# Two more score steps in the ring at the end of a pass of a Mamba, attention and experts kernel

## What is computed

```python
# L0: tokens by 64 channels -> 128 inner channels, 16 states, a scan along 1024 tokens
xh = silu(causal_conv_k2(xh, conv_w, conv_b)); dt = softplus(dt_low @ W_dt + b_dt)
h = exp(dt * A) * h + dt * B * x;  y = einsum('bdn,bn->bd', h, C) + xc * D
x = silu(group_norm((y * silu(z)) @ W_out)) + x
# L1 attention, 1024 tokens, 8 heads of 8, causal
att = softmax(mask(q @ k.T * scale)); t = t + (att @ v) @ w_proj
# L1 experts: top 2 of 8
t = t + sum over the top 2 of p_e * (ln(t) @ expert_w[e] + expert_b[e])
```

## Time and profile before

| | |
|---|---|
| median of 3 runs | 1405.29 us (1405.14 to 1409.21) |
| the profiled execution | 1405.26 us, of which its span is 1403.4 us |
| busy over the span | PE 74%, DVE 80%, ACT 49%, POOL 35% |
| granted TensorE clock, mean | 0.856 of full speed |
| largest group of DVE | L979 `row_max`, 352 instructions, 328.8 us |
| share of the chain that ended last | DVE 39%, PE 28%, of it L979 16% |

### The profile page before, as it was taken

One profiled execution on the slowest core, in us unless ns is written; L12 is line 12 of the kernel. 1 busy time (PEld: TensorE's weight loads), 2 busy tenths in 40 slices (PEclk: granted clock), 3 DMA queues, 4 the chain that ended last, 5 costly groups with the idle time before them and its releaser, 6 DMA issues.

```text
span 1403.4 us, 16864 instructions
## 1 busy us (share of the span) xinstructions
PE 1032.5 (74%) x6132; PEld 431.9 (31%) x6132; DVE 1116.6 (80%) x1398; ACT 684.2 (49%) x1178; POOL 487.1 (35%) x257
## 2 busy tenths in 40 slices
PE   3255325858886898779877998689868976986984
PEld 1001101323333333323333334233333333433442
DVE  5695359898899998999899989998999987258235
ACT  3324212438644774367446654576437702740660
POOL 3262336335442543353255334444425421000000
PEclk9557556979987999889987998899879997999895
DMA  2640583154425333534335433543154321120000
GB/s 45 165 120 31 124 169 82 40 143 123 100 64 141 97 80 90 134 91 110 72 96 125 117 82 81 123 115 81 51 135 104 81 58 41 35 50 1 2 16 8
DMA packets 40937, 120.25 MB, mean 86 GB/s; under 512 B 9222, under 2 KB 9610, under 8 KB 38475
## 3 DMA queue, kind: packets, MB, share of 16 engines
q1 hardware_dynamic: 27030, 68.83, 21.1%
q10 hardware_dynamic: 13824, 50.34, 14.4%
HBM read 95.65 MB, written 17.20 MB: 80 GB/s over the span
## 4 chain that ended last, share of the span: by engine, by line
DVE 39%; PE 28%; issue 9%; ACT 3%; POOL 2%; DMA 1%; DVEq 0%; ACTq 0%; SPq 0%
DVE row_max L979 16%; DVE state L1045 8%; PE ps L1436 6%; PE ps L1421 5%; DVE drive L1054 4%; PE ps L1304 3%; PE ps L1216 2%; PE ps L1196 2%; PE ps L1405 2%; ACT probs L866 2%; PE ps L1201 2%; DVE moe L1136 2%; PE ps L1207 1%; PE ps L1353 1%; PE ps L1424 1%
## 5 line engine op out<-in xcount | busy, mean ns | idle before, releaser
L711 POOL TENSOR_TENSOR read<-state,c_rep 128x1024 f32<-128x1024 f32 x128 | 311.3, 2434 | 365.5 <-DVE state L1045 271.9
L866 ACT ACTIVATE probs<-ps 128x512 f32<-128x512 f32 (+3 forms) x768 | 327.2, 499 | 109.2 <-PE ps L1424 79.1
L979 DVE TENSOR_REDUCE row_max<-ps 128x1 f32<-128x640 f32 (+7 forms) x352 | 328.8, 985 | 39.0 <-PE ps L1308 38.0
L1045 DVE TENSOR_TENSOR_SCAN state<-decay,drive 128x1024 f32<-128x1024 f32 x96 | 265.3, 2764 | 1.6 <-DVE drive L1054 1.2
L1421 PE MATMUL ps<-q_stack,k_stack 128*128 128x512 bf16 (+3 forms) x768 | 214.6, 345 | 65.4 <-DVE drive L1054 28.7
L1304 PE MATMUL ps<-k_stack,q_stack 128*128 128x512 bf16 (+3 forms) x704 | 200.0, 365 | 72.0 <-DVE row_max L979 70.0
L821 ACT ACTIVATE decay<-decay,a_scale 128x1024 f32<-128x1024 f32 x128 | 147.1, 1154 | 100.8 <-DMA decay<-dt_dram 100.8
L1353 PE MATMUL ps<-u_rows,pick 128*128 128x512 bf16 x256 | 113.1, 466 | 100.3 <-DVE state L1030 73.7
L1436 PE MATMUL ps<-probs,v_aug 128*32 128x512 f32 (+3 forms) x1536 | 168.2, 510 | 8.8 <-ACT probs L866 3.7
L1421 PEld LDWEIGHTS ps<-q_stack,k_stack 128*128 128x128 bf16 x768 | 75.9, 100 | 253.7 <-ACT probs L866 65.1
L1054 DVE TENSOR_TENSOR drive<-ps,b_rep 128x512 f32<-128x512 f32 x192 | 127.7, 678 | 21.0 <-PE ps L1353 19.3
(11 more groups left out here) (184 smaller groups left out, 1262.7 us busy)
## 6 DMA issues: line engine op xcount, KB each, us to landing
decay<-dt_dram ACTq DMA_DIRECT2D x96, 512.0 KB, 4.7
decay<-dt_dram SPq DMA_DIRECT2D x32, 512.0 KB, 6.1
q_stack<-q_parts_dram SPq DMA_DIRECT2D x48, 192.0 KB
k_stack<-k_parts_dram SPq DMA_DIRECT2D x48, 192.0 KB
u_rows<-read SPq DMA_DIRECT2D x96, 64.0 KB, 2.0
k_parts_dram<-read SPq DMA_DIRECT2D x40, 128.0 KB, 2.4
dt_dram<-read SPq DMA_DIRECT2D x8, 512.0 KB, 2.6
q_parts_dram<-read SPq DMA_DIRECT2D x24, 128.0 KB, 2.3
```

Source lines behind the costliest of these rows:

```text
L711: pool.tensor_tensor(read[:, k % (2 * NG), :], state[:, k % 2, :], c_rep[:, :], ALU.mult)\
L866: act.activation(probs[:, e % (2 * QUAD), 0:w], bank_of(("scores", e))[:, 0:w], ACT.Exp, scale=SCALE).then_inc(exped.sem, 1)
L979: dve.tensor_reduce(row_max[:, i, h0:h0 + nh], scores[:, :, 0:P * (i + 1)], AX.X, ALU.max, negate=True).then_inc(row_maxed.sem, 1)
L1045: dve.tensor_tensor_scan(state[:, k % 2, :], decay[:, k % DECAYS, :], drive[:, k % 3, :], 0.0, ALU.mult, ALU.add).then_inc(scanned.sem, NH)
```

## The change

`EARLY_STEPS` gets two steps more, block 2 with head 0 and block 2 with head 1, 384 columns each. The score half loses the step of block 2 with heads 0 and 1 (768 columns), so it has 43 steps where it had 44. The two new steps stand behind the last values and ahead of `heads_to_tokens(3)`. The next pass begins with two folds, the convolution, two folds and then score step 5. In `beside` nothing but the folds' steps is renumbered, so all else there stands one step earlier in the row of blocks. In the rounds half, unit 13 goes from round 9 to round 10, and f's two sets of transposes `xn_t` go from round 10 to round 8.

```diff
-        EARLY_STEPS = [(0, 0, 4), (1, 0, 2), (1, 2, 2)]
+        EARLY_STEPS = [(0, 0, 4), (1, 0, 2), (1, 2, 2), (2, 0, 1), (2, 1, 1)]
+        BEFORE_VALUES = 3
...
-                                     if quad or i > 1]
+                                     if quad or i > 2 or (i == 2 and h > 1)]
...
-        UNITS_IN = (4, 0, 2, 1, 2, 0, 2, 0, 2, 1, 2, 2, 0, 1, 2, 0, 1, 0, 1, 1, 2, 1, 2, 1, 1, 1, 0, 0)
+        UNITS_IN = (4, 0, 2, 1, 2, 0, 2, 0, 2, 0, 3, 2, 0, 1, 2, 0, 1, 0, 1, 1, 2, 1, 2, 1, 1, 1, 0, 0)
...
-        TURNS = ((0, "attn_t", 0), (1, "attn_t", 1), (2, "proj", 0), (10, "xn_t", 0), (10, "xn_t", 1),
+        TURNS = ((0, "attn_t", 0), (1, "attn_t", 1), (2, "proj", 0), (8, "xn_t", 0), (8, "xn_t", 1),
...
-                        ((1, 1), c, convolution), ((0, 2, 4, 5), p, last_folds), ((6, 8), c, gate_projection),
+                        ((1, 1), c, convolution), ((0, 0, 2, 3), p, last_folds), ((6, 8), c, gate_projection),
...
                     if p:
-                        for n in range(NEARLY):
+                        for n in range(BEFORE_VALUES):
                             early_scores(n)
                     if b:
                         add_values(NKEY - 1)
+                    if p:
+                        for n in range(BEFORE_VALUES, NEARLY):
+                            early_scores(n)
+                    if b:
                         heads_to_tokens(len(GROUPS) - 1)
```

## The result

| | before | changed |
|---|---|---|
| median of six runs | 1405.22 us (1404.09 to 1409.21) | 1397.07 us (1395.00 to 1399.73) |
| ratio, 95% interval | | 0.9937 (0.9918 to 0.9956) |
| profiled execution, span | 1405.26, 1403.4 | 1399.73, 1398.0 |
| DVE and PE busy, clock | 80%, 74%, 0.856 | 80%, 73%, 0.854 |

The direction was the forecast's, the size that of the most favourable rival, or more. The profiled execution of the changed kernel is the slowest of its six, so the two traces differ by 5.5 us only. One pair of traces must therefore not be read as the effect, and most of what follows is about telling the change from chance.

What follows compares the result with a forecast made beforehand. DVE, busy 137.0 of 150.0 us, was taken to set the pass, so only its waits could be won. Pass 3 +2.9, passes 4 to 8 -3.5, pass 9 -0.5, pass 10 -1.85: -2.95 from 1405.26, 1402.3 us, range 1398 to 1408.

Steps and rivals of the forecast that it cites:

- the most favourable rival: Whole kernel: clock in pass 3 rises as early as before, later gains come in full; -6.65, 1398.6 us; chance 0.25.
- the price in pass 3: Head of pass 3: new steps wait for scans, folds queue behind, `gate_scan` 2.2 late; 2.9 us lost (1.3 to 5.8).
- Passes 9 and 10: Score halves only: pass 9 gains 0.5 us, pass 10 gains 1.85; nothing was counted for their rounds.
- The 1.85 in pass 10's score half: Pass 10: first step of block 3 starts 1.1 earlier, value projection's wait shrinks by 0.75; 1.85 us gained (1.1 to 1.9).
- if it takes that long again it rises at 248.4: Head of pass 3: PE's clock again rises only after 5.58 us of unbroken work, making `gate_scan` 2.2 late.
- Head of passes 4 to 8: `gate_scan` starts 1.08 us earlier, but the first step of block 3 only 0.20 earlier.
- the cover by ACT's copy: Head of passes 4 to 8: new steps' 0.5 us of PE fit the 0.70 gap while ACT copies the sums.
- Score half, 0.35 a pass: Passes 4 to 8: chain from `gate_group_norm` starts 1.35 earlier, leaving 0.35 us a pass gained (0.1 to 0.60).
- Rounds half, 0.35 a pass from the wait of 0.70: Passes 4 to 8: moving unit 13 removes unit 16's 0.70 wait, unit 14 comes 0.35 later; 0.35 us a pass gained.
- All that can be won is won: Whole kernel: pass 3 costs only 1.4, passes 4 to 8 gain 0.60 and 0.50 each; -6.65, 1398.6 us; chance 0.25.
- The gains are handed back: Passes 4 to 8: later DVE waits grow by what is won, DVE's work unchanged; +0.55, 1405.8 us; chance 0.2.
- The transposes block the ring: Round 10, passes 4 to 8: units 13, 14, 15 each 0.6 late; +6.2 in all, 1411.5 us; chance 0.1.

Runs made afterwards that it cites:

- r1: The changed kernel run again, nothing altered: 1397.38 us, ratio 0.9949 to the kernel before.
- r15: The changed kernel run once more, nothing altered: 1397.29 us, ratio 0.9960 to the kernel before.
- r9: The kernel before, unaltered, run for a second trace: one time, 1401.61 us.
- r11: The changed kernel plus products that nobody reads (the filling) in three PE waits of passes 9 and 10: 1390.48 us, ratio 0.9902.
- r10: The kernel before plus products that nobody reads (the filling) in three PE waits of passes 9 and 10: 1400.55 us, ratio 0.9972.
- r8: The changed kernel with all five early steps ahead of the last values: 1399.47 us, ratio 0.9960.
- r7: The changed kernel with the numbers of `beside`, except folds, convolution and `gate_scan`, one higher: 1403.99 us, ratio 0.9998.
- r3: The changed kernel without the rounds half's moves (unit 13 back in round 9, `xn_t` back in round 10): 1397.68 us, ratio 0.9959.
- r14: The changed kernel with unit 13 back in round 9, `xn_t` staying in round 8: 1396.34 us, ratio 0.9952.
- r6: The kernel before with half of POOL's product left out, plus unit 13 in round 10 and `xn_t` in round 8: 1373.03 us, ratio 0.9787.

## Why the prediction was right or wrong

By stretch, the difference of means between traces of the changed kernel (the first, r1, r15) and of the kernel before (the first, r9). r11 and r10 are taken in where the filling can't have changed a stretch. The forecast is cut at the same places: its 1.08 for the head of pass 4 falls into the second row (0.73 - 1.08), and that of pass 9 into the third.

| | measured, us | forecast |
|---|---|---|
| start to `gate_scan` of pass 3 | +1.0 | +2.2 |
| from there to that of pass 4 | +0.3 | -0.35 |
| from there to that of pass 9 | -3.6 | -3.5 |
| from there to the third division of pass 9 | -0.7 | +0.6 |
| from there to the cast of pass 10 | -0.8 | -1.85 |
| rounds of pass 10 to the end | -2.4 | 0 |
| sum of the unrounded rows | -6.1 | -2.95 |

The three comparisons of medians say -8.15, -6.65 and -6.6; the interval of the last, 3.8 to 7.6, holds the 6.1, and the rest can't be placed with so few traces. The forecast missed in the rows outside passes 4 to 8: it put the rounds of passes 9 and 10 at nothing and the price in pass 3 too high. Inside passes 4 to 8 the number is right and its reason wrong.

- **Passes 9 and 10, the term that was missing.** The rounds of both passes stood in the sum with nothing, though PE sets them. xn_t in round 8 gives 0.38 in each. From the cast of pass 10 to the first division it is 1.7 less, at a granted clock of 0.71 to 0.84 where before had 0.65; by r10 and r11 that part is the clock's. The 1.85 in pass 10's score half was right where the clock stayed at 1.00 (1.58 from the third division on) and came to nothing where it fell in that half (0.88 to 0.94), in seven of eleven traces with the early steps.
- **Pass 3's head.** The mechanism was right (steps wait for scans, folds queued behind them, first fold behind 243). The step that failed is "if it takes that long again it rises at 248.4": in the first trace the convolution at 246.87 already ran at full clock, and the price was 1.23, near the lower bound of 0.7. Over many traces it drowns in what the clock does there anyway.
- **Head of passes 4 to 8.** "1.08 earlier" is 1.36, since folds in a row are cheaper; the cover by ACT's copy held, and r8 prices it at 0.44 a pass where 0.5 was said.
- **Score half, 0.35 a pass.** Head and score half together give 1.36 less 1.04 that goes again between `gate_scan` and the cast: 0.32. The argument was wrong all the same. r7 shows that the chain's earlier start gives 0.1 there and 0.4 behind the cast, which the prediction had not in its sum.
- **Rounds half, 0.35 a pass from the wait of 0.70.** This step failed outright. The wait ahead of unit 16 went, and nothing was won (r3 and r14 take as long as the changed kernel in passes 4 to 8): the scan behind it grew by 0.79. Its cause was wrong too: in r14 the wait is gone with unit 13 where it was. Two errors cancelled: 0.35 for moves that gave nothing, and nothing for the 0.4 that the shift gave behind the cast. That passes 4 to 8 came out at 3.6 against 3.5 is luck.
- **The rivals.** "All that can be won is won" came closest in size, for other reasons. "The gains are handed back" was right about the wait of 0.70 alone, and named the wrong taker: not a later wait but a longer scan. It held DVE's work to be the same, and so did not ask whether an instruction could become longer. "The transposes block the ring" asked for waits of more than 0.9 ahead of L1054 in round 10: in pass 6 they sum to 0.56 in the changed kernel, and to 1.26 in r6.

## What to carry to other kernels

A wait that is taken away can come back as a longer instruction behind it: before a wait is put into a sum, compare the mean of the next instruction of the same form with its shortest, and look which engine runs beside it. Work that is pulled forward needs both the hole that it leaves for and the chain behind it moved up; each alone showed nothing here. And where PE waits at a known place while its clock falls, products that nobody reads, put into that wait, were worth 6.9 us in the changed kernel, about as much as the change itself.

## What the runs showed of the hardware

- A DVE scan of 1024 columns took 2.28 us alone and 2.14 or 2.15 plus the overlap when POOL's product of two operands in SBUF was already running, up to 4.32 in the first trace of before. Halving that product (2.36 to 1.27) made the kernel 34 us faster.
- The other way round it is POOL that stands still: five scans of that trace began 0.56 to 0.58 ahead of a product and take 2.28, and the product takes 3.87 or 3.88 instead of 2.36.
- The granted clock changes at other places in other executions of one kernel: nine of the changed kernel lie between 1391.84 and 1400.65. In passes 4 to 8 the stretches at clock 1.00 repeat to 0.03 in two traces of before.
- Unread products in three waits of PE (2.67, 0.76 and 1.50 us) held the clock at 1.00 through 19.93 us that took 20.94 to 24.37 without them, in traces of the two kernels.
